# Seven half-size products for the gate and up projections of one more batch, and a new timetable

## The chip, the cores and the metric

The kernel runs on one core of a Trainium2 chip. The metric is the device time of one execution in microseconds (us). TensorE (PE) multiplies matrices into the eight banks of PSUM, VectorE (DVE), ScalarE (ACT) and GpSimd (POOL) do elementwise work, SyncE (SP) issues DMAs. Each engine takes its instructions in the order in which the program lists them; semaphores are the only tie between engines.

## The reference

The kernel computes a decoder layer of three sublayers for 4 batches of 512 tokens with 512 features, each followed by a residual sum and a layer norm: causal attention with 16 heads, the WKV recurrence over the context (a scan over the tokens, for which `k` is the first sublayer's output and `v` the context), and a gated feed-forward of 2048 hidden features with integer weights less 128, times a scale for each row.

```python
x = _layernorm(x + _L0_attn_ref(x, Wqkv, bqkv, Wo, bo))
x = _layernorm(x + _L0_xattn_ref(4, 512, 512, w, u, x, ctx_2048))
g = einsum('bsh,ih->bsi', x, Wg);  u = einsum('bsh,ih->bsi', x, Wu)
x = _layernorm(x + einsum('bsi,hi->bsh', silu(g) * u, Wd))
```

## The kernel before, in words

Every matrix product takes the float32 activations as a high and a low float16 part. `timetable()` (line 219) writes one list of pieces of work, by slots whose numbers stand in tables at the top of the file (`QK_AT`, `WKV_AT`, `WS_AT` and so on), and each engine's block walks through that list and issues its own share of every piece. So the list sets the order on every engine, and a piece whose input is late holds up all that stands behind it on its engine. Slots below 1000 lie in the attention stage. Slot 1000 + 20 b + i is in the feed-forward of batch b, after hidden tile i (0 to 15), and 1016 + 20 b + t after its y product t (0 to 3). Slots 1000 to 1007 count as 1008: the first eight tiles of batch 0 are done inside attention. A tile makes 2 ticks of the list, a y product 4, and `WAIT_IN` says how many ticks after its start a step of a chain is listed.

The feed-forward runs batch by batch: the 16 hidden tiles, then four y products of 32 matmuls.

Batches 0 and 1, the plain way: for each tile 8 matmuls of 512 columns for gate and 8 for up (`gate_up`, line 1133). ScalarE takes silu (line 1426), VectorE multiplies it with the up product (`hf`, line 1662), ScalarE and GpSimd split the result into `hh` (line 1441) and `hl` (line 1938). Their activations are `x2h` and `x2l` (lines 1359 and 1645).

Batches 2 and 3 (`SEVEN`), by seven products: the gate and up weights are stacked to one matrix and the 2 by 2 block product is done with 7 products of half-size blocks (in Winograd's form of Strassen's scheme) in place of 8. For a pair m of tiles (8 pairs) each product is 8 matmuls of 256 columns (`product`, line 1160). They need sums of weights (`weight_sum`, line 946: `WSUM`, four sums of two halves) made once, and sums of the quarters of the activations made for each batch (`quarters`: ScalarE's `x_full`, line 1364, VectorE's `x_sum`, line 1677, ScalarE's high parts, line 1377, VectorE's low parts, line 951). ScalarE copies three partial sums of each pair out of PSUM (`snap`, line 1401: snap1 before product 6, snap6 before product 7, snap5 before product 3), VectorE adds (`c11`, `c12`, `c22`, lines 1685, 1691, 1697), ScalarE takes silu (line 1408), VectorE closes with `hfb` and `hfa` (line 964), and ScalarE makes `hh` (line 1414).

Beside this run the WKV chains of later batches, four per batch: exponentials on ScalarE (lines 1323 and 1326), products on GpSimd (lines 1901 to 1918), the two scans, ekv and the division on VectorE (lines 1621, 1629, 1616, 1634), and a logarithm and an exponential (lines 1339 and 1341). Silu and these use different ACT tables, so ScalarE loads a table at each change (lines 1330, 1408, 1426). Then come `yt` with its residual and statistics (lines 1593, 1579, 1581), the second norm (line 1607) and the transposes `x2t` (line 1120). The context of a batch is loaded by SyncE (`load_ct`) to `CTS[b]`. After a y product VectorE scales and adds it (lines 1707, 1713), and ScalarE normalises it (line 1346) before SyncE writes it out (line 2088).

## Time and profile before

| what | us |
|---|---|
| median of 3 runs (lowest, highest) | 708.04 (707.57, 708.64) |
| profiled execution's own time | 711.66 |
| span of its profile | 709.9 |
| attention, to about | 375 |
| rest of batch 0's tiles and its four y products, to | 455.3 |
| batch 1's tiles, to | 515 |
| batch 1's y products, to | 544.3 |
| batch 2's tiles, to | 597.8 |
| batch 2's y products, to | 627.1 |
| batch 3's tiles, to | 676.2 |

A stage ends where TensorE issues the first matmul of the next. Matmuls overlap in the pipeline, so the pace of a stage is read from the starts of its matmuls and not from the length of one. Idle time stands in brackets behind the instruction that it precedes, with the one that ended it.

### The profile page before, as it was taken

Reading aid. Unit: us, or ns where it says so; the run is one execution under the profiler, and the core shown is the slowest. Engines: PE = TensorE matmul, PEld = TensorE weight load, DVE = VectorE, ACT = ScalarE, POOL = GpSimd, SP = SyncE. Lnnn points to the kernel's source line nnn. Section 1 sums busy time; section 2 is a strip of 40 time slices with the busy share of each in tenths; the row PEclk is TensorE's granted clock in tenths of the full one; section 3 lists DMA queues with packets and bytes.
Section 4 is the critical chain, followed back from the end, with each engine's and each line's share of the span. In section 5 each row is a group of like instructions: output and inputs, shape, how many; then the busy total and the mean of one; then the engine's idle time right before and its main releaser. Section 6 shows DMA issues by size and latency. Waiting matters only on the chain.

```text
span 709.9 us, 12525 instructions
## 1 busy us (share of the span) xinstructions
...
## 2 busy tenths in 40 slices
...
GB/s 239 249 218 235 217 145 135 98 75 79 124 102 78 38 85 163 120 143 16 8 120 60 1 0 75 16 31 0 1 1 44 17 1 2 30 31 1 1 16 45
DMA packets 45024, 54.33 MB, mean 77 GB/s; under 512 B 5921, under 2 KB 33825, under 8 KB 44961
## 3 DMA queue, kind: packets, MB, share of 16 engines
...
q10 hardware_dynamic: 432, 0.39, 0.2%
...
## 4 chain that ended last, share of the span: by engine, by line
PE 61%; DVE 13%; ACT 10%; POOL 5%; issue 5%; DMA 4%; SPq 1%; POOLq 0%; DVEq 0%; ACTq 0%
PE psb L1160 12%; PE psb L1133 8%; PE psb L996 6%; PE psb L1184 5%; PE psb L1182 5%; PE psb L1104 4%; PE psb L1072 4%; PE psb L1027 4%; DVE ee L1530 3%; PE psb L1039 3%; PE psb L1056 3%; DVE x L1607 2%; PE psb L1120 2%; PE psb L1083 2%; ACT L1330 1%
## 5 line engine op out<-in xcount | busy, mean ns | idle before, releaser
L1530 DVE CUSTOM_DVE_ANT_0 ee<-psb,mask,clip 128x512 f32<-128x512 f32 (+3 forms) x256 | 131.3, 542 | 24.9 <-PE psb L1039 22.3
L1278 ACT ACTIVATE ee<-ee,nm 128x512 f32<-128x512 f32 (+3 forms) x256 | 142.2, 560 | 1.4 <-DVE nm L1530 1.4
L1938 POOL TENSOR_TENSOR hl<-ring,hh 128x512 f16<-128x512 f32 x64 | 80.1, 1264 | 86.7 <-ACT hh L1414 57.3
L1288 ACT ACTIVATE ee<-psb 128x256 f32<-128x256 f32 (+1 forms) x192 | 94.6, 523 | 31.0 <-PE psb L1056 21.0
L1182 PE MATMUL psb<-wd,hh 128*128 128x512 f16 x240 | 91.0, 379 | 0.0
L1184 PE MATMUL psb<-wd,hl 128*128 128x512 f16 x240 | 91.0, 379 | 0.0
L1868 POOL TENSOR_SCALAR_AFFINE_SELECT ee<-ee 128x256 f32<-128x256 f32 x128 | 56.8, 452 | 60.7 <-ACT ee L1288 59.9
L1039 PE MATMUL psb<-ks,qs 128*128 128x512 f16 (+3 forms) x256 | 72.5, 305 | 8.3 <-DVE nm L1530 6.1
L1056 PE MATMUL psb<-qs,ks 128*128 128x128 f16 (+3 forms) x256 | 60.1, 306 | 9.6 <-ACT ee L1288 7.5
L996 PE MATMUL psb<-xh,wqk 128*128 128x512 f16 x240 | 61.8, 385 | 1.7 <-POOL xh L1830 1.2
L1885 POOL TENSOR_TENSOR rs<-ve,half 128x1 f32<-128x1 f32 (+1 forms) x24 | 20.5, 854 | 72.0 <-DVE ve L1599 71.7
L1278 ACT ACTIVATION_READ_ACCUMULATOR ee<-ee,nm 128x1 f32 x256 | 51.0, 199 | 0.0
L1133 PE MATMUL psb<-x2h,wg 128*128 128x512 f16 x128 | 48.6, 380 | 0.8 <-ACT ring L1426 0.5
L1133 PE MATMUL psb<-x2h,wu 128*128 128x512 f16 x128 | 48.5, 379 | 0.0
L1133 PE MATMUL psb<-x2l,wu 128*128 128x512 f16 x128 | 48.5, 379 | 0.0
L1133 PE MATMUL psb<-x2l,wg 128*128 128x512 f16 x128 | 48.5, 379 | 0.0
L1039 PEld LDWEIGHTS psb<-ks,qs 128*128 128x128 f16 x256 | 25.0, 99 | 35.6 <-DVE nm L1530 11.5
L1441 ACT ACTIVATE hh<-ring 128x512 bf16<-128x512 f32 x32 | 20.2, 630 | 30.6 <-DVE ring L1662 30.6
L1056 PEld LDWEIGHTS psb<-qs,ks 128*128 128x128 f16 x256 | 23.6, 99 | 32.1 <-ACT ee L1288 14.8
L1072 PE MATMUL psb<-ee,v 128*32 128x128 f32 (+3 forms) x512 | 37.8, 435 | 0.7 <-POOL ee L1868 0.6
L1184 PEld LDWEIGHTS psb<-wd,hl 128*128 128x128 f16 x240 | 23.4, 98 | 27.3 <-POOL hl L1938 0.2
L1182 PEld LDWEIGHTS psb<-wd,hh 128*128 128x128 bf16 x240 | 23.4, 98 | 27.2
...
## 6 DMA issues: line engine op xcount, KB each, us to landing
...
parts<-qhl SPq DMA_DIRECT2D x16, 256.0 KB, 2.2
parts<-khl SPq DMA_DIRECT2D x16, 256.0 KB, 2.2
x<-in_x SPq DMA_DIRECT2D x4, 1024.0 KB, 6.8
ct<-in_ctxT SPq DMA_DIRECT2D x4, 1024.0 KB, 5.1
out<-x SPq DMA_DIRECT2D x16, 256.0 KB, 2.0
xt<-in_xT SPq DMA_DIRECT2D x14, 256.0 KB, 3.4
```

Source lines behind the costliest of these rows:

```text
L996: mm = e.matmul(PSB[:, bk, :], wt[:, k, c0:c0 + P], xt[:, k, :], start=(p == 0 and k == 0), stop=(p == 2 and k == T - 1))
L1039: e.matmul(PSB[:, bank["score", H, i], 0:w], heads(n, "q")[:, h, i * P:(i + 1) * P], heads(n, "k")[:, h, 0:w], start=True, stop=True).then ...
L1056: mm = e.matmul(PSB[:, bk, o:o + (T - j) * P], heads(n, "k")[:, h, j * P:(j + 1) * P], heads(n, "q")[:, h, j * P:S], start=True, stop=True)
L1072: mm = e.matmul(PSB[32 * h:32 * h + 32, bk, j * P:S], VV[:, b % 2, j, g * P + 32 * h:g * P + 32 * h + 32], ET[(4 * n + h) % ET_SLOTS][:, T ...
L1133: mm = e.matmul(PSB[:, bk, :], wt[:, k, it * P:(it + 1) * P], xt[:, s, k, :], start=(k == 0 and xt is x2h), stop=(k == T - 1 and xt is x2l))
L1160: mm = e.matmul(PSB[:, bk, k * HALF_S:(k + 1) * HALF_S], weights(j, kk, 2 * m + k), moving(b, j, kk, low), start=(unit is not None and k + ...
L1182: e.matmul(PSB[:, bk, :], HS[it][0][:, t * P:(t + 1) * P], wd[:, it, :], start=(it == 0), stop=False)
L1184: mm = e.matmul(PSB[:, bk, :], HS[it][1][:, t * P:(t + 1) * P], wd[:, it, :], start=False, stop=(it == IT - 1))
L1278: e.activation(dst, dst, ACT.Exp, bias=NM[:, n % 4, col:col + 1], scale=-1.0, accum_out=DEN[:, n % 4, col:col + 1]).then_inc(sem("exp"), 1)
L1288: e.activation(ET[H % ET_SLOTS][:, base:base + width], PSB[:, bank["turn", H, item], 0:width], ACT.Exp, scale=SC).then_inc(sem("et"), 1)
L1530: e.tensor_tensor_reduce(E[H % E_SLOTS][:, EOFF[i]:EOFF[i] + w], PSB[:, bank["score", H, i], 0:w], MASK[:, S - w:S], -SC, CLIP[:, i:i + 1] ...
L1938: e.tensor_tensor(HS[it][1][:], pair(b, it // 2)[:, it % 2, :] if b in SEVEN else ring(b, it)[1], HS[it][0][:], ALU.subtract).then_inc(sem ...
```

## The change

Batch 1 joins `SEVEN`, so its 256 matmuls of 512 columns become 448 of 256 columns, with the sums and closings described above. For this the buffers are dealt anew: the quarters of batch 1 lie over `CT` (`XE[1]`, and its snap5 in `CT[:, 3, :]`), so the context of batch 3 goes to `X[0]`, batch 0's result, and is loaded only when that has been written out. The fourth sum of weights goes to `QS3` and `KS3` and no longer over `X[0]`. The sums of weights are listed in slots 1010 to 1018 (they were in 1021 to 1036), and for that the last attention output product of batch 3 in slot 1010 (it was in 1013). All tables of slots are new; those of the feed-forward stand in full below, those of attention cut to a few.

```diff
-SEVEN = (2, 3)
+SEVEN = (1, 2, 3)
-W_SPLIT = (10, 14, 17, 19)
-V0_AT = (0, 12)
+W_SPLIT = (9, 13, 13, 15)
+V0_AT = (1, 14)
-V_AT = {1: (56, 57, 58, 66), 2: (119, 127, 137, 145), 3: (178, 191, 192, 203)}
+V_AT = {1: (55, 58, 60, 69), 2: (118, 126, 139, 146), 3: (178, 191, 192, 206)}
...
-WAIT_IN = {'r1': 1, 'norm': 3, 'ek': 0, 'scan_q': 0, 'scan_p': 9, 'seed': 10, 'refine': 3, 'divide': 6, 'r2': 0,
-           'x2h': 0, 'x2l': 0, 'norm2': 7}
+WAIT_IN = {'r1': 1, 'norm': 4, 'ek': 0, 'scan_q': 0, 'scan_p': 11, 'seed': 11, 'refine': 3, 'divide': 8, 'r2': 0,
+           'x2h': 2, 'x2l': 11, 'norm2': 7}
...
-WKV_AT = {(0, 0): 124, (0, 1): 136, (0, 2): 144, (0, 3): 162, (1, 0): 204, (1, 1): 215, (1, 2): 259, (1, 3): 270,
-          (2, 0): 1003, (2, 1): 1013, (2, 2): 1017, (2, 3): 1018, (3, 0): 1020, (3, 1): 1031, (3, 2): 1035, (3,
-          3): 1040}
-YT_AT = {0: (172, 178, 185, 191), 1: (1013, 1014, 1015, 1016), 2: (1026, 1027, 1028, 1029), 3: (1045, 1046, 1047,
-         1049)}
-X2_AT = {0: (222, 225, 226, 233), 1: (1018, 1018, 1018, 1018), 2: (1036, 1036, 1037, 1037), 3: (1057, 1057, 1057,
-         1057)}
-WO_IN = (7, 8, 9, 13)
+WKV_AT = {(0, 0): 123, (0, 1): 135, (0, 2): 143, (0, 3): 162, (1, 0): 204, (1, 1): 215, (1, 2): 259, (1, 3): 270,
+          (2, 0): 1001, (2, 1): 1015, (2, 2): 1017, (2, 3): 1020, (3, 0): 1023, (3, 1): 1032, (3, 2): 1036, (3,
+          3): 1038}
+YT_AT = {0: (172, 179, 185, 191), 1: (1012, 1013, 1013, 1015), 2: (1029, 1032, 1033, 1033), 3: (1043, 1045, 1045,
+         1047)}
+X2_AT = {0: (226, 226, 230, 235), 1: (1017, 1018, 1018, 1018), 2: (1036, 1036, 1036, 1036), 3: (1055, 1055, 1055,
+         1056)}
+WO_IN = (7, 8, 9, 10)
...
-WS_AT = {1: (1025, 1028), 2: (1026, 1035), 3: (1021, 1023), 4: (1033, 1036)}
+WS_AT = {1: (1010, 1011), 3: (1014, 1017), 2: (1012, 1015), 4: (1014, 1018)}
...
     def last(b, t):
         add("norm", 2, b, t, t + 1)
         add("out", b, t)
+        if (b, t) == (0, T - 1):
+            add("load_ct", 3)
...
-    CTS = [CT, CT, CT2, CT]
+    CTS = [CT, CT, CT2, X[0]]
...
-            4: (X0H[:, 0:I], X0H[:, I:2 * I])}
-    XE = {2: CT2[:].bitcast(F16).rearrange("p t n -> p (t n)"), 3: X[1][:].bitcast(F16).rearrange("p t n -> p (t n)")}
+            4: tuple(w[:].rearrange("p k n -> p (k n)") for w in (QS3, KS3))}
+    XE = {1: CT[:].bitcast(F16).rearrange("p t n -> p (t n)"), 2: CT2[:].bitcast(F16).rearrange("p t n -> p (t n)"), 3: X[1][:].bitcast(F16).rearrange("p t n -> p (t n)")}
-    SNAP5 = [CT2[:, 3, :], YS[:, 1, :]]
+    SNAP5 = {b: (c[:, 3, :], YS[:, 1, :]) for b, c in ((1, CT), (2, CT2), (3, CT2))}
...
         if j == 4:
-            q.wait_ge(sem("out0"), 16 * T)
+            q.wait_ge(*by_turned(NG - 1))
...
+                elif b == 3:
+                    sp.wait_ge(sem("out0"), 16 * T)
                 elif b:
-                    sp.wait_ge(*by("yt", b // 2, T - 1))
+                    sp.wait_ge(*by("yt", 0, T - 1))
```

## Rows read from the trace of the kernel before

**Rows 1.** Busy us (xinstructions) of each engine by stretch.

```profile
core 0: us, PE busy (x) PEld busy (x) DVE busy (x) ACT busy (x) POOL busy (x), PEclk, DMA share, GB/s
0.00:375.00 375.00, 344.58 (x2157) 178.79 (x2158) 289.41 (x855) 310.95 (x866) 234.00 (x356) 0.98 0.48 127
...
399.60:455.30 55.70, 55.70 (x281) 27.87 (x278) 40.50 (x64) 30.95 (x47) 32.92 (x30) 1.00 0.07 25
455.30:515.00 59.70, 59.02 (x286) 28.21 (x286) 42.94 (x54) 37.83 (x51) 42.98 (x35) 1.00 0.04 14
515.00:544.30 29.30, 29.30 (x146) 14.24 (x144) 22.60 (x32) 13.65 (x20) 15.75 (x16) 1.00 0.05 19
544.30:597.80 53.50, 51.90 (x470) 45.62 (x469) 43.99 (x78) 35.86 (x60) 22.96 (x21) 1.00 0.03 11
...
627.10:676.20 49.10, 49.10 (x450) 43.66 (x449) 30.62 (x57) 30.06 (x52) 14.45 (x14) 1.00 0.02 6
```

**Rows 2.** Timeline of TensorE: start us, length us, line, operation.

```profile
500.65 0.38 PE L1133 MATMUL psb<-x2h,wg 128*128 128x512 f16 x1
...
514.46 0.60 PE L1120 MATMUL psb<-ident,x 128*128 128x128 f32 x4
...
627.09 0.27 PE L1160 MATMUL psb<-x2h,wg 128*128 128x256 f16 x1
...
676.09 0.38 PE L1182 MATMUL psb<-wd,hh 128*128 128x512 f16 x1
```

**Rows 3.** Waits of 455 to 515: us in total, times, longest.

```profile
DVE ekv L1616 <- ACT ek L1323: 2.7, 1, 2.7
DVE ct L1634 <- POOL ct L1918: 2.3, 1, 2.3
```

**Rows 4.** TensorE's idle times in batch 2's products (timeline).

```profile
...
555.68 0.39 PE L1160 MATMUL psb<-ct,woh 128*128 128x256 f16 x2 [0.32 <-ACT ys L1401]
...
559.81 0.39 PE L1160 MATMUL psb<-ct,s2a 128*128 128x256 f16 x2 [0.46 <-ACT snap L1401]
...
563.42 0.39 PE L1160 MATMUL psb<-ct,woh 128*128 128x256 f16 x2 [0.82 <-ACT ys L1401]
```

**Rows 5.** Timeline of ScalarE in the same stretch.

```profile
552.51 1.28 ACT L1408 ACT_TABLE_LOAD   x1
553.81 1.33 ACT L1408 ACTIVATE ring<-ring,g 128x512 f32<-128x512 f32 x2
...
555.64 1.28 ACT L1330 ACT_TABLE_LOAD   x1
```

**Rows 6.** Groups of VectorE in 455.3 to 515: xcount | busy, mean ns.

```profile
L1662 DVE SCALAR_TENSOR_TENSOR ring<-ring,c,psb 128x512 f32<-128x512 f32 x14 | 10.4, 745 | 9.4 <-ACT ring L1426 9.3
```

**Rows 7.** One line's instructions: the sums of weights, first and dearest.

```profile
L946 DVE TENSOR_TENSOR woh<-wg,wu x1: 2079/2079/2079, 472.0 to 472.0; 128x2048 f16<-128x2048 f16 x1
L946 DVE TENSOR_TENSOR wol<-wg,wu x1: 1217/1217/1217, 480.8 to 480.8; 128x2048 f16<-128x2048 f16 x1
```

**Rows 8.** The same view: quarter sums, their low parts, the low part removed.

```profile
L1677 DVE TENSOR_TENSOR ring<-ring x6: 682/692/693, 532.7 to 615.7; 128x512 f32<-128x512 f32 x6
...
L951 DVE TENSOR_TENSOR x2l<-ring,x2h x4: 1218/1218/1221, 535.4 to 618.2; 128x1024 f16<-128x1024 f32 x4
...
L1645 DVE SCALAR_TENSOR_TENSOR x2l<-psb,x2h x8: 678/684/691, 309.8 to 454.5; 128x512 f16<-128x512 f32 x8
```

**Rows 9.** Timeline of VectorE: its last step behind batch 0's third y product.

```profile
450.73 0.15 DVE L1599 TENSOR_SCALAR ve<-mv 128x1 f32<-128x1 f32 x1
```

**Rows 10.** The page's DMA issues: xcount, KB each, median us to landing.

```profile
ct<-in_ctxT SPq DMA_DIRECT2D x4, 1024.0 KB, 5.1
out<-x SPq DMA_DIRECT2D x16, 256.0 KB, 2.0
```

**Rows 11.** Groups of VectorE in 544.3 to 597.8.

```profile
L964 DVE SCALAR_TENSOR_TENSOR ring<-ring,c,psb 128x256 f32<-128x256 f32 x14 | 6.0, 471 | 0.5 <-PE psb L1160 0.4
...
L964 DVE SCALAR_TENSOR_TENSOR ring<-ring,c,ys 128x256 f32<-128x256 f32 x6 | 2.9, 524 | 0.0
```

More of the change, by code:

```diff
@@ L117 @@
-WO_IN = (7, 8, 9, 13)
-WD_AT = (257, 257, 258, 261)
-ZERO_IN = (1, 4, 6, 8, 9, 9, 9, 9, 9, 10, 10, 11, 11, 13, 13, 17)
-WS_AT = {1: (1025, 1028), 2: (1026, 1035), 3: (1021, 1023), 4: (1033, 1036)}
+        2, 'ek': 1, 'scan_q': 2, 'scan_p': 14, 'seed': 6, 'refine': 8, 'divide': 13, 'r2': 1, 'x2h': 0, 'x2l': 1,
+        'expand': 4}
+WAIT_IN = {'r1': 1, 'norm': 4, 'ek': 0, 'scan_q': 0, 'scan_p': 11, 'seed': 11, 'refine': 3, 'divide': 8, 'r2': 0,
+           'x2h': 2, 'x2l': 11, 'norm2': 7}
+PIECE_AT = {'load_second': 33, 'small': 70, 'split_wo': 47, 'load_ds': 180}
@@ new lines @@
+WU_AT = (41, 47, 48, 48)
+WU_ZERO = (61, 121, 121, 143)
+WG_AT = (202, 214, 221, 233)
+WG_ZERO = (220, 223, 242, 243)
+REST_AT = (7, 28, 96, 15)
+BO_AT = (53, 97, 128, 183)
+XLOAD = {1: (2, 4, 26, 30), 2: (62, 65, 88, 90), 3: (128, 132, 147, 162)}
+XSPLIT = {1: (24, 28, 32, 33), 2: (83, 84, 94, 97), 3: (145, 159, 162, 165)}
+WKV_AT = {(0, 0): 123, (0, 1): 135, (0, 2): 143, (0, 3): 162, (1, 0): 204, (1, 1): 215, (1, 2): 259, (1, 3): 270,
+          (2, 0): 1001, (2, 1): 1015, (2, 2): 1017, (2, 3): 1020, (3, 0): 1023, (3, 1): 1032, (3, 2): 1036, (3,
+          3): 1038}
@@ L361, in residual @@
                 late(wait("norm"), lambda: add("norm", 1, b, 0, T))
-                if b < 2:
-                    add("load_ct", 2 * b + 1)
+                if b == 0:
+                    add("load_ct", 1)
         for c in range(T):
@@ L1370, in x_part_high @@
                 act.wait_ge(*by("xt", b, k))
-            if k < 2:
+            if k < 2 and b == 1:
+                act.wait_ge(*by_put(NG - 1, "q"))
+                act.wait_ge(*by_put(NG - 1, "k"))
+            elif k < 2:
                 act.wait_ge(*by_gate_up(b - 2))
-            elif b == 2:
+            elif b < 3:
                 act.wait_ge(*by("yt", b, T - 1))
```

70 lines of the change are left out of this document (27 added, 43 removed), and 18 rows, old and new, of the table TURN_AT.

## The prediction, made before the changed kernel was run

> **What bounds the kernel now.** I read the busy time by stretch first. From 399.6 us, where the last tiles of batch 0 run, TensorE is busy in every microsecond but 0.7 in batch 1's tiles and 1.6 in batch 2's, at a granted clock of 1.00, the level of 2.4 GHz [rows 1]. So from there to the end the time is the number of matmul columns, and each microsecond of matmuls taken away counts, if no other engine takes TensorE's place. Up to 375 us TensorE is idle for 375.0 - 344.6 = 30.4 us, in many small waits [rows 1]. The second thing to see is how near the others are: VectorE has 40.5 of 55.7 us and then 42.9 of 59.7 (73% and 72%), but 44.0 of 53.5 (82%) in batch 2's products, where TensorE begins to wait [rows 1]. The engine that the change loads is the one that is second now.
>
> The profiled execution took 711.66 us, its span is 709.9, and the median of the runs is 708.04. All terms below are differences inside the feed-forward; I make the sum against 711.66 and take off the 3.62 between it and the median.
>
> **The products.** Before, 64 matmuls of 512 columns go from 500.65 to 514.46, 0.2158 us each; in batch 3 448 of 256 columns go from 627.09 to 676.09, 0.1094 us each [rows 2]. Batch 1 has 256 of the first kind, 55.24 us, and gets 448 of the second, 49.00 us: **-6.24**. The 0.7 us of idle time in its tiles [rows 1] belongs to the plain way (a tile waited for a bank) and goes: **-0.66**, as 59.70 - 59.02. Together -6.90. The y products, the transposes and their places between the tiles stay as many.
>
> **Stalls inside batch 1's products.** Three products of each pair wait for a copy by ScalarE. With one WKV chain in its way batch 2 lost 0.32, 0.46 and 0.82, that is 1.60 us [rows 4]: ScalarE went to load a table, 1.28 us, for silu, and again for the logarithm, while the copies stood behind [rows 5]. Batch 1's stage has three chains: (2,3) at slot 1020, (3,0) at 1023 and (3,1) at 1032. At 1.60 each that is 4.8; (2,3) begins while TensorE waits for the quarters anyway (next part), and the end of (3,1) moves into the y products, since its start behind tile 12 leaves 7 ticks in the tiles and its second scan is listed 11 after its start. So I take two, **+3.2**. The lower end is one, 1.6. The upper end is given by VectorE and is worked out with the second rival.
>
> ScalarE's own load is no bound: 37.8 us before, of which the new way replaces some 19 (silu and high parts) by batch 3's 30.1 [rows 1], so 49 in about 55.
>
> The Trainium skill ("ScalarE: Activation LUTs", section "What ACT_TABLE_LOAD costs") puts a drain of 1.38 us on top of the 1.28 us of each change of table, 2.66 in all. The row speaks otherwise: the load begins at 552.51 and the silu behind it starts at 553.81, 0.02 us after its end [rows 5]. By the page each of the four changes of two chains would cost 1.38 more and the term would be 8.7 in place of 3.2; I go by the row.
>
> **The start of batch 1's products.** New before the first product are 2 ScalarE steps and five of VectorE. Behind batch 0's third y product VectorE is free at 450.9 [rows 9]. Then come the last sum of weights (1.22) [rows 7], four sums of quarters (4 x 0.69) and the first low part (1.22) [rows 8]: 456.1, where TensorE is ready at 455.3. That is 0.8. Product 6, fourth in the order, waits for snap1, which waits for all low parts, since the last of them reads the tile that snap1 overwrites: 456.1 + 2 x 1.22 + 0.68 [rows 8] + a copy of 0.6 (ScalarE's mean in batch 3, 30.1 us over 52 [rows 1]) = 459.8, and three products of 8 x 0.1094 bring TensorE there at 458.7. That is 1.1. Together **+2.0**. Not less than 0: the quarters could be ready in time if VectorE ran ahead. Not more than 4.0, if the sums of weights listed in tiles 10 to 15 leave VectorE some 2 us behind.
>
> **The sums of weights.** Eight instructions of VectorE, two of 2.1 and six of 1.2 to 1.4, 11.7 us [rows 7], move from batch 1's and its y products' slots to 1010 to 1018. VectorE is idle for 15.2 us of the 55.7 there [rows 1], and they lie in that: 0 by themselves. Without that cover they delay the last `hf` of batch 0, then `hh` and `hl`, and y(0,0), which reads the pairs in order; that is held in the two ends of the start.
>
> **Batch 2's products.** Chain (3,3) starts two slots earlier, among y products, though its logarithm is still listed at the second tile of batch 2. I take half of its 1.60 as gone: **-0.8**, ends 0 and -1.6.
>
> **Batch 3's context.** It now waits until batch 0 is written out. In SyncE's queue it stands behind the write of y(0,3), and nothing is queued there that another engine wants earlier. Batch 0's last norm is listed after tile 1 of batch 1, about 465 us; the write takes 2.0 and the load 5.1 [rows 10], so it lands at about 473. Its reader, ekv of chain (3,0), is listed after tile 3: 457 + 2 x 6.1 + 0.4 = 470, and ScalarE's two exponentials, 1.3 us, as two silus [rows 5], and the chain before it come first: 471 to 473. **0**, with 4.0 as the upper end: VectorE would stand in its queue before `c11`, and TensorE two products behind it.
>
> **Attention.** Its pieces are the same in number and length, only slots move by up to nine. It has 30.4 us of idle time in which a move can gain or lose [rows 1], and I see no row that gives a sign: **0**, ends -3 and +3.
>
> **The sum.** -6.24 - 0.66 + 3.2 + 2.0 - 0.8 = -2.50. 711.66 - 2.50 = 709.16 for the profiled execution, less 3.62: **705.5 us** for the median.
>
> **The rivals.**
>
> *The cover holds.* The start costs nothing, and the stage no more than batch 2's did, 1.6: 708.04 - 6.90 + 1.6 - 0.8 = 701.9. For it: batch 3's 448 products ran with no gap at all [rows 1, 2]. Against it: no chains ran beside them, and VectorE had 30.6 of 49.1.
>
> *VectorE becomes the bound* (the slower side). Its work from 399.6 to 515 was 40.5 + 42.9 = 83.4 us [rows 1]. Off go 14 `hf` of 0.745 (10.4) [rows 6], four low parts of 0.68 (2.7) [rows 8] and the second scan and division of (3,1), about 2. On come the closings, batch 3's 30.6 [rows 1] less 2.5 for the y product's remainder in it, 28.1; four sums of quarters and the low parts, 2.8 + 4.3 [rows 8]; and the two sums of weights that stood behind 515, 2.6 [rows 7]. That makes 106.1, where TensorE has 115.4 - 6.9 = 108.5 left. In my forecast the stretch lasts 113.7, so VectorE may be idle for 7.6 us of it. It had forced waits of 2.7 for exponentials and 2.3 for GpSimd in batch 1's stage alone [rows 3], and in batch 2's products it was idle for 9.5 of 53.5 [rows 1]. At that share it would be idle for 10.6 in the stage, and with 1.8 more before it the stretch lasts 118.5: 3.1 more than before, less 0.8 for batch 2, 710.3. It decides from 10 us of idle time on. For it: the sum itself. Against it: much of the idle time in batch 2 was waiting for TensorE, which a late VectorE doesn't do. Its far end, everything from 399.6 at 18% idle, is beyond 713.
>
> *Batch 3's context is late.* Priced at 3 in addition to the forecast, 708.5, the same as before.
>
> *VectorE and GpSimd block each other.* Batch 1 has GpSimd busy for 43.0 us [rows 1]. Sixteen `hfb` and four low parts read two tiles of SBUF each. Its mean instruction there is 43.0 / 35 = 1.23 us [rows 1]. If each of the twenty had to wait for half of one, three times in four, that is 20 x 0.61 x 0.75 = 9, and the time 714.5. Against it: in batch 2 the `hfb` that read `YS` took 524 ns on average where `hfa`, which reads PSUM, took 471 [rows 11]; at that rate it is 1 us in all, hidden in my 3.2. The Trainium skill ("SBUF — State Buffer", section "Who interferes with whom") has such a rule: an instruction of VectorE with two SBUF inputs and one of GpSimd exclude each other for their whole length. The measured 53 ns show it to be rare here.
>
> *The attention's new slots decide*: 3 us either way, 702.5 or 708.5.
>
> **How the numbers follow.** Forecast 0.42 (704 to 707: 0.37 faster, 0.05 same), cover holds 0.15 (faster), VectorE the bound 0.22 (0.18 slower, 0.04 same), late context 0.10 (0.08 same, 0.02 slower), blocking 0.04 (slower), attention 0.07 (0.03, 0.02, 0.02). 0.2% is 1.4 us, about what a measurement can tell from no change here. Faster 0.55, same 0.19, slower 0.26. The range goes from 701.0, just under the case where the cover holds, to 711.0, just over the central price of the VectorE case; the tail of that case, blocking and an attention that gains on top of a full cover stay outside. Cases of both signs hold much of the chance; the forecast's own range is 704 to 707.
>
> **What would show it.** The spacing of the products in batch 1: 0.1094 us. Idle time before line 1160 between about 455 and 512, ended by ScalarE's copies, 3 to 4 us, most of it near table loads; the second rival shows VectorE over 93% busy there, with waits ended by lines 1685 to 1697 or 1677 and 951. The first product comes 0 to 2 us after the last y matmul of batch 0, and no gap inside y(0,0). A VectorE wait for the DMA into `x` before ekv shows the third rival. TensorE's idle time before 375 should be 27 to 33 us. The forecast is wrong if batch 1's stage, first product to first y matmul, isn't 53 to 58 us long, or if attention moves by more than 3 us.

## The result, and the profile after

| | before | after |
|---|---|---|
| median of 4 runs each (lowest, highest) | 707.81 (707.48, 708.64) | 731.1 (730.18, 731.4) |
| profiled execution's own time | 711.66 | 731.01 |
| span of its profile | 709.9 | 729.3 |

The ratio is 1.0306, with a 95% interval of 1.0281 to 1.033: the change makes the kernel 23.3 us slower, where 705.5 was predicted. The two traces differ by 19.4; the other 3.9 is that the profiled run of before lay 3.9 over its own median, while that of after is at its median. All medians are of executions at the usual clock; one execution of e3, at a mean granted clock of 0.56, took 1150.26 us and is left out.

First the stages, from the first matmul of one to the first of the next, read from TensorE's timeline; the 3.95 us of waiting ahead of batch 1's first product is counted with its tiles. "Idle" is TensorE's, "half" is the time at a granted clock of 1.2 GHz.

| stage | before: us (idle, half) | after: us (idle, half) | difference |
|---|---|---|---|
| to y(0,0) | 424.5 | 422.9 | -1.6 |
| y products of batch 0 | 30.9 (0, 0) | 30.0 (0, 0) | -0.9 |
| batch 1's tiles | 59.6 (0.5, 0) | 71.2 (14.1, 10.2) | +11.6 |
| y products of batch 1 | 29.4 (0, 0) | 34.5 (2.2, 3.4) | +5.2 |
| batch 2's tiles | 53.5 (1.6, 0) | 59.8 (5.9, 6.8) | +6.4 |
| y products of batch 2 | 29.4 (0, 0) | 28.1 (0, 0) | -1.3 |
| batch 3 | no change | no change | 0 |

In the wake of a change to one stage, three stages lost. From y(0,0) to the end the kernel before takes 285.4 us and the kernel after 306.4, so the feed-forward lost 21.0. The feed-forward repeats (e10, which has that of the kernel before, takes 285.5 us); what lies before y(0,0) doesn't. With the old tables of attention it took 424.5, 421.5 and 421.4 us in the profiled runs of the kernel before, e2 and e8, with the new ones from 419.5 to 426.4. The other 2.3 us of the 23.3 is within that scatter.

The busy time of the engines by stretch, of the kernel after (us, then each engine's busy time and instructions, granted clock of TensorE, DMA share, GB/s), says that no engine was full over a whole stage:

```profile
core 0: us, PE busy (x) PEld busy (x) DVE busy (x) ACT busy (x) POOL busy (x), PEclk, DMA share, GB/s
0.00:375.00 375.00, 347.81 (x2171) 181.10 (x2172) 290.90 (x856) 314.18 (x870) 236.38 (x358) 0.98 0.47 127
399.60:452.30 52.70, 52.68 (x265) 26.21 (x263) 47.15 (x66) 26.05 (x39) 36.36 (x27) 1.00 0.02 6
452.30:524.10 71.80, 57.75 (x480) 48.52 (x479) 57.84 (x89) 51.34 (x77) 38.50 (x35) 0.93 0.08 27
524.10:558.40 34.30, 32.03 (x154) 15.93 (x152) 26.06 (x37) 16.50 (x24) 16.28 (x17) 0.95 0.02 9
558.40:618.40 60.00, 54.13 (x479) 47.50 (x478) 44.40 (x79) 34.01 (x57) 24.62 (x23) 0.94 0.04 14
```

In batch 1's tiles TensorE has 57.8 of 71.8 us, VectorE 57.8, ScalarE 51.3, GpSimd 38.5: the fullest stands at 81%. What a reader should look for then is not the busiest engine of the stage but what each waited for. TensorE's timeline, its longest waits from batch 1 to batch 2's first pairs (start, length, operation; in brackets the idle time before it and what ended it):

```profile
456.84 0.27 PE L1161 MATMUL psb<-x2h,wg 128*128 128x256 f16 x1 [3.95 <-DVE x2l L952]
...
475.19 0.39 PE L1161 MATMUL psb<-ct,s2a 128*128 128x256 f16 x2 [1.18 <-ACT snap L1399]
...
478.80 0.39 PE L1161 MATMUL psb<-ct,woh 128*128 128x256 f16 x2 [0.82 <-ACT ys L1399]
...
487.14 0.61 PE L1161 MATMUL psb<-ct,s2a 128*128 128x256 f16 x2 [4.67 <-ACT snap L1399]
...
520.33 0.39 PE L1161 MATMUL psb<-ct,woh 128*128 128x256 f16 x2 [1.69 <-ACT ys L1399]
...
531.61 0.39 PE L1183 MATMUL psb<-wd,hh 128*128 128x512 f16 x1 [1.35 <-ACT hh L1412]
...
566.91 0.58 PE L1161 MATMUL psb<-ct,s2a 128*128 128x256 f16 x2 [5.54 <-ACT snap L1399]
```

All but the first end with one of ScalarE's copies (`snap`, line 1399 now) or parts. So the next view is ScalarE's timeline ahead of 487.14, then that of VectorE, on which ScalarE waited, and GpSimd's beside it:

```profile
482.84 1.15 ACT L1412 ACTIVATE hh<-ring 128x512 bf16<-128x512 f32 x2 [4.09 <-DVE ring L965]
484.01 1.28 ACT L1331 ACT_TABLE_LOAD   x1
485.30 0.63 ACT L1340 ACTIVATE qs_<-ek 128x512 f32<-128x512 f32 x1
485.96 0.63 ACT L1342 ACTIVATE qs_<-qs_ 128x512 f32<-128x512 f32 x1
486.50 0.58 ACT L1399 ACTIVATE snap<-psb 128x512 f32<-128x512 f32 x1
```

```profile
474.10 1.24 DVE L1614 TENSOR_TENSOR ekv<-ek,x 128x512 f32<-128x512 f32 x1 [1.12 <-ACT ek L1324]
475.26 2.17 DVE L1619 TENSOR_TENSOR_SCAN qs_<-ew,ek 128x512 f32<-128x512 f32 x1
477.36 0.66 DVE L1683 TENSOR_TENSOR ring<-psb,snap 128x512 f32<-128x512 f32 x1
477.94 2.14 DVE L965 SCALAR_TENSOR_TENSOR ring<-ring,c,ys 128x256 f32<-128x256 f32 x2
480.01 1.75 DVE L1632 SCALAR_TENSOR_TENSOR ct<-ek,ct 128x512 f32<-128x512 f32 x1
481.68 0.68 DVE L1689 TENSOR_TENSOR ring<-psb,ys 128x512 f32<-128x512 f32 x1
482.29 0.86 DVE L965 SCALAR_TENSOR_TENSOR ring<-ring,c,psb 128x256 f32<-128x256 f32 x2
```

```profile
474.75 3.64 POOL L1936 TENSOR_TENSOR hl<-ring,hh 128x512 f16<-128x512 f32 x2
...
478.51 1.29 POOL L1899 TENSOR_TENSOR x<-ek,x 128x512 f32<-128x512 f32 x1
479.88 1.33 POOL L1903 TENSOR_TENSOR ek<-ek,qs_ 128x512 f32<-128x512 f32 x1
```

This is one chain through three engines. VectorE takes ekv and a scan of chain (3,0) and the division of chain (2,3) between the closings of a pair; so `hfa` is late (482.29), ScalarE's `hh` stands first in its queue and waits 4.09 us for it, and behind `hh` stand a table load, the logarithm, the exponential and only then the copy for which TensorE waits. The order of the lists is one part of it. The other is that VectorE had no gap from 474.10 to the closing at 482.29: in these 8.2 us it was full. And four of its groups there took longer than usual, each with GpSimd at work beside it: ekv 1.24 for a median of 0.69, the scan 2.17 for 1.22, two `hfb` 2.14 for 0.96, the division 1.75 for 0.71. By these rows I estimate 3.7 us of lengthening, most of the 4.09. The sum at 477.36, with an input in PSUM and GpSimd at work beside it too, took its usual 0.66. I wrote at the top that semaphores are the only tie between the engines; by these rows they are not. e12 below says how much of it is due to GpSimd's chain work.

In batch 2 it is the same in other clothes. ScalarE's and GpSimd's timelines ahead of 566.91:

```profile
564.29 0.63 ACT L1340 ACTIVATE qs_<-ek 128x512 f32<-128x512 f32 x1 [6.03 <-POOL ek L1903]
564.95 0.63 ACT L1342 ACTIVATE qs_<-qs_ 128x512 f32<-128x512 f32 x1
565.49 0.80 ACT L1347 ACTIVATE x<-x,shift,rs 128x512 f32<-128x512 f32 x1
566.19 0.57 ACT L1399 ACTIVATE snap<-psb 128x512 f32<-128x512 f32 x1
```

```profile
552.15 1.27 POOL L1908 TENSOR_TENSOR x<-x,ps 128x512 f32<-128x512 f32 x1 [7.95 <-DVE ps L1627]
...
562.67 1.59 POOL L1903 TENSOR_TENSOR ek<-ek,qs_ 128x512 f32<-128x512 f32 x1
```

GpSimd waited 7.95 us for the second scan of chain (3,2), which stands behind the sums of quarters in VectorE's queue; the sum of chain (3,3), which now starts two slots sooner, comes 10 us later (562.67), and its logarithm is listed ahead of the first `snap`. The distance of the second scan, 11 now, is not the reason: with the old 9 GpSimd waits 7.23 us at the same place (e13).

### The profile page after: what moved, and what is told of

It reads as the page before. It is cut to its first block and busy times, and to the rows that moved or that the text cites. A ratio compares the mean times of both kernels' runs of the same rounds, so it can differ in the third digit from the quotient of the medians.

```text
span 729.3 us, 13011 instructions
## 1 busy us (share of the span) xinstructions
PE 674.1 (92%) x4482; PEld 403.8 (55%) x4482; DVE 540.2 (74%) x1264; ACT 508.0 (70%) x1167; POOL 398.5 (55%) x508
## 5 line engine op out<-in xcount | busy, mean ns | idle before, releaser
L1289 ACT ACTIVATE ee<-psb 128x512 f32<-128x512 f32 (+1 forms) x192 | 94.4, 523 | 26.3 <-PE psb L1057 17.0
L1883 POOL TENSOR_TENSOR rs<-ve,half 128x1 f32<-128x1 f32 (+1 forms) x24 | 22.3, 929 | 63.0 <-DVE ve L1597 62.8
L1412 ACT ACTIVATE hh<-ring 128x512 bf16<-128x512 f32 x48 | 27.5, 620 | 36.5 <-DVE ring L965 35.3
L1161 PE MATMUL psb<-x2h,wg 128*128 128x256 f16 x192 | 45.3, 276 | 3.9 <-DVE x2l L952 3.9
L1161 PE MATMUL psb<-x2l,wg 128*128 128x256 f16 x192 | 45.3, 276 | 0.0
L1040 PEld LDWEIGHTS psb<-ks,qs 128*128 128x128 f16 x256 | 24.9, 100 | 34.7 <-DVE nm L1528 11.2
L1185 PEld LDWEIGHTS psb<-wd,hl 128*128 128x128 f16 x240 | 23.5, 98 | 29.4 <-POOL hl L1936 2.5
L1183 PEld LDWEIGHTS psb<-wd,hh 128*128 128x128 bf16 x240 | 23.5, 98 | 28.8 <-ACT hh L1412 1.8
L1683 DVE TENSOR_TENSOR ring<-psb,snap 128x512 f32<-128x512 f32 x24 | 16.5, 689 | 27.4 <-PE psb L1161 23.3
L997 PEld LDWEIGHTS psb<-xh,wqk 128*128 128x128 f16 x240 | 22.5, 98 | 24.8 <-POOL xh L1828 2.3
```

The source lines that it names most:

```text
L997: mm = e.matmul(PSB[:, bk, :], wt[:, k, c0:c0 + P], xt[:, k, :], start=(p == 0 and k == 0), stop=(p == 2 and k == T - 1))
L1040: e.matmul(PSB[:, bank["score", H, i], 0:w], heads(n, "q")[:, h, i * P:(i + 1) * P], heads(n, "k")[:, h, 0:w], start=True, stop=True).then ...
L1161: mm = e.matmul(PSB[:, bk, k * HALF_S:(k + 1) * HALF_S], weights(j, kk, 2 * m + k), moving(b, j, kk, low), start=(unit is not None and k + ...
L1183: e.matmul(PSB[:, bk, :], HS[it][0][:, t * P:(t + 1) * P], wd[:, it, :], start=(it == 0), stop=False)
L1185: mm = e.matmul(PSB[:, bk, :], HS[it][1][:, t * P:(t + 1) * P], wd[:, it, :], start=False, stop=(it == IT - 1))
L1289: e.activation(ET[H % ET_SLOTS][:, base:base + width], PSB[:, bank["turn", H, item], 0:width], ACT.Exp, scale=SC).then_inc(sem("et"), 1)
```

## The experiments

Each kernel is the one after with the edit shown, unless another is named, and each ratio is to the kernel before on the same chip. "Tiles 1" is the stage of batch 1's tiles, with the wait ahead of its first product, "tiles 2" that of batch 2's. Where a kernel computes less, its expectation says which part. Microseconds against the kernel after are taken from its 731.1, which was measured apart; the median of the kernel before lay between 707.8 and 709.9 in the several groups of runs, so such a difference is good to a microsecond or two.

**e1_slots_plain.** The slots without the seven products.

```diff
-SEVEN = (1, 2, 3)
+SEVEN = (2, 3)
```

> The changed kernel with batch 1 done the plain way again (SEVEN = (2, 3)), all else of the change kept: new slots, sums of weights at 1010 to 1018, batch 3's context in X[0]. Theory L (load): what costs is the load of batch 1's copies, closings and quarters on VectorE and ScalarE beside the WKV chains. Then this runs at 706 to 711 us, and batch 1's tiles take about 60 us with under 1.5 us of idle TensorE. Theory S (slots): the new slots put the chains, the sums of weights and chain (3,3)'s logarithm in bad places whatever batch 1 does. Then batch 2's products keep some 6 us of idle time and slow clock, and the time is 715 us or more.

Measured 722.47, ratio 1.0196 (1.0147 to 1.0245). But part of it was made by the experiment: the plain way's low parts were listed with the wait of the new one (`x2l` 11), behind the scaling of y(0,3), which made TensorE wait 5.73 us with a lower clock behind it. e5 repeats it without that and is 7.6 us shorter.

**e2_old_slots_seven.** All the old tables except `WS_AT` and `WO_IN`, with the seven products.

```diff
-          (2, 0): 1001, (2, 1): 1015, (2, 2): 1017, (2, 3): 1020, (3, 0): 1023, (3, 1): 1032, (3, 2): 1036, (3,
-          3): 1038}
+          (2, 0): 1003, (2, 1): 1013, (2, 2): 1017, (2, 3): 1018, (3, 0): 1020, (3, 1): 1031, (3, 2): 1035, (3,
+          3): 1040}
...
```

> The changed kernel (batch 1 by seven products) with all tables of slots of the kernel before, except WS_AT and WO_IN, which have to be the new ones. Theory L: 725 us or more, batch 1's products with over 10 us of idle TensorE, since the work beside them is the same. Theory S: the old places are the better ones, 703 to 712 us.

741.97, ratio 1.0476 (1.0419 to 1.0534). Tiles 1 take 77.2 us with 17.2 idle, and y(0,0) waits 5.98 us for the down weights that ScalarE converts. Tiles 2 are as in the kernel before (53.5, 1.6 idle). So the new timetable doesn't make tiles 1 slow, since they are slower still in the old one, but what tiles 2 lost comes with the new one; e5 says so too.

**e3_one_table.** Chains of batches 2 and 3 without changes of table.

```diff
-            e.activation(SEED, EK2S[c % 2][:], ACT.Ln).then_inc(sem("seed"), 1)
+            e.activation(SEED, EK2S[c % 2][:], ACT.Ln if b < 2 else ACT.Copy).then_inc(sem("seed"), 1)
...
```

> The changed kernel with the exponentials and the logarithm of the chains of batches 2 and 3 replaced by identity and copy of the same size (so their values are wrong), so that ScalarE needs no change of table beside silu. If the table loads in ScalarE's queue are what holds back the copies out of PSUM: 8 to 14 us less than the changed kernel, 717 to 723. If VectorE's queue (closings, scans, quarters) is the bound and ScalarE only passes its lateness on: 727 to 731.

723.54, ratio 1.02 (1.0151 to 1.0249): 7.6 us of the 23.3. The wait in the middle of tiles 1 is hardly shorter, 4.31 in place of 4.67:

```profile
484.74 0.39 PE L1161 MATMUL psb<-ct,s2a 128*128 128x256 f16 x2 [4.31 <-ACT snap L1401]
```

My forecast had put the price of a chain on the table loads. That is a third of it.

**e4_chains_later.** The four chains of batch 3 later: tiles 1 have one chain beside them in place of three.

```diff
-          (2, 0): 1001, (2, 1): 1015, (2, 2): 1017, (2, 3): 1020, (3, 0): 1023, (3, 1): 1032, (3, 2): 1036, (3,
-          3): 1038}
+          (2, 0): 1001, (2, 1): 1015, (2, 2): 1017, (2, 3): 1020, (3, 0): 1036, (3, 1): 1038, (3, 2): 1042, (3,
+          3): 1047}
...
```

> The changed kernel with the chains of batch 3 later: (3,0) to (3,3) at 1036, 1038, 1042, 1047 in place of 1023, 1032, 1036, 1038, and yt of batch 3 at 1051 to 1054. Batch 1's products then have one chain beside them in place of three. Theory L: batch 1's stage gets 7 to 10 us shorter, of which batch 2's products, which get more of a chain, give back 2 to 4: 722 to 727. If the cost is the late quarters and the start of batch 1's products, or the closings by themselves: 729 to 733.

744.56, ratio 1.0491 (1.0447 to 1.0534). Tiles 1 fell from 71.2 to 59.4, and tiles 2 rose from 59.8 to 85.6. The waits that are left in tiles 1 behind the first product, with one chain, (2,3), beside them:

```profile
469.25 0.39 PE L1161 MATMUL psb<-ct,woh 128*128 128x256 f16 x2 [0.33 <-ACT ys L1399]
473.38 0.39 PE L1161 MATMUL psb<-ct,s2a 128*128 128x256 f16 x2 [0.46 <-ACT snap L1399]
476.99 0.39 PE L1161 MATMUL psb<-ct,woh 128*128 128x256 f16 x2 [0.82 <-ACT ys L1399]
```

These are the 1.6 us of the forecast, wait by wait: a lone chain costs in batch 1 what it cost in batch 2. The two further ones of the kernel after bring the idle time behind the first product from 1.6 to 10.1. In tiles 2, where one chain's first scan lay (558.9) and at whose start or within which three do now (543.3, 564.5 and 585.3), the idle time rises from 5.9 to 23.5. Not all of this is crowding: the last wait, 6.8 us, is for the second norm of batch 3, whose inputs this edit also made later.

**e5_slots_plain_x2.** e1 with the plain way's old waits.

```diff
-SEVEN = (1, 2, 3)
+SEVEN = (2, 3)
-            'x2h': 2, 'x2l': 11, 'norm2': 7}
+            'x2h': 0, 'x2l': 0, 'norm2': 7}
...
```

> As e1_slots_plain (batch 1 the plain way, all new slots), but batch 1's x2h and x2l are listed straight behind their transposes, as in the kernel before; the quarters of batches 2 and 3 keep their new place. In e1_slots_plain TensorE waited 5.7 us before batch 1's first tile for x2l, which the new WAIT_IN lists behind y(0,3)'s scaling, and the clock fell for 6.8 us. If that is an artefact of doing batch 1 plainly in these slots: 722.5 falls by 7 to 9 us to 713 to 716, and what is left above the kernel before is batch 2's 5.5 us of idle time and slow clock, due to the slots alone. If batch 1's first tile is late for another reason: 719 us or more.

714.87, ratio 1.0072 (1.0044 to 1.01). So some 5 us (by the ratio) to 6.5 (by the medians) are the new slots' own; behind y(0,0) its trace is 5.6 longer than that of the kernel before. Tiles 2 take 60.9 (53.5 before) and batch 1's y products 31.1 (29.4), 9.2 more, and the other stages gain the rest back. The wait is the very one of the kernel after, with batch 1 in the plain way:

```profile
549.53 0.58 PE L1161 MATMUL psb<-ct,s2a 128*128 128x256 f16 x2 [5.55 <-ACT snap L1402]
```

The seven products in batch 1, in these slots, cost the other 16.2 (15.4 behind y(0,0) in the traces).

**e6_last_chain.** Only chains (3,2) and (3,3) put back to where they were.

```diff
-          (2, 0): 1001, (2, 1): 1015, (2, 2): 1017, (2, 3): 1020, (3, 0): 1023, (3, 1): 1032, (3, 2): 1036, (3,
-          3): 1038}
+          (2, 0): 1001, (2, 1): 1015, (2, 2): 1017, (2, 3): 1020, (3, 0): 1023, (3, 1): 1032, (3, 2): 1035, (3,
+          3): 1040}
```

> The changed kernel with only two chains put back to their old slots: (3,2) at 1035 and (3,3) at 1040 in place of 1036 and 1038. Theory S for batch 2: the logarithm of (3,3), which ScalarE reaches before batch 2's first copy and for which it waits 6.0 us on GpSimd, causes the 5.5 us of idle time and the 6.8 us of slow clock there. Then batch 2's products take 53 to 56 us in place of 59.6, and the time is 724 to 728. If batch 2 is late since batch 1's work spills over into it: no change, 730 to 733.

734.48, ratio 1.0356 (1.0333 to 1.0379). The 5.54 before `snap` went, and 5.65 came further on, where a transpose waits for the division of the late chain. The wait moved and did not shrink.

```profile
578.48 0.87 PE L1121 MATMUL psb<-ident,x 128*128 128x128 f32 x3 [5.65 <-DVE x L1632]
```

**e7_short_after** and **e8_short_before.** Every instruction of the chains of batches 2 and 3 on 8 columns in place of 512, in the kernel after and in the kernel before: as many instructions, waits and places, but almost no work.

```diff
+    def W(b):
+        return S if b < 2 else 8
...
-            e.activation(SEED, EK2S[c % 2][:], ACT.Ln).then_inc(sem("seed"), 1)
+            e.activation(SEED[:, 0:W(b)], EK2S[c % 2][:, 0:W(b)], ACT.Ln).then_inc(sem("seed"), 1)
...
```

> The changed kernel with every instruction of the WKV chains of batches 2 and 3 on 8 columns in place of 512 (the rest of the recurrence is left out): their number, order, waits and table loads stay, their work nearly goes. Compared with e8_short_before, the same cut in the kernel before. Theory L1 (the chains' work beside the closings is what costs): the change then saves, e7 is 2 to 6 us under e8. Theory L2 (closings, copies and quarters are too much for VectorE and ScalarE by themselves): e7 is above e8 by 5 us or more.

> The kernel before with the chains of batches 2 and 3 on 8 columns (the rest of the recurrence is left out). The plain tiles and y products hid them, but for the 1.6 us in batch 2's products: 705 to 708 us under either theory.

e7: 710.68 (10 runs), ratio 1.0027 (1.0007 to 1.0047). e8: 706.99 (10 runs), 0.9972 (0.9955 to 0.9988). The chains' work costs 20.4 us in the kernel after and 1 to 2 in the kernel before. Without it the change costs 3.7.

**e9_short_one_table.** e7 and e3 together.

```diff
+    def W(b):
+        return S if b < 2 else 8
...
-            e.activation(SEED, EK2S[c % 2][:], ACT.Ln).then_inc(sem("seed"), 1)
+            e.activation(SEED[:, 0:W(b)], EK2S[c % 2][:, 0:W(b)], ACT.Ln if b < 2 else ACT.Copy).then_inc(sem("seed"), 1)
...
```

> e7_short_after (the changed kernel, chains of batches 2 and 3 on 8 columns) without their table changes too (identity and copy in place of exponential and logarithm; that part of the work is left out). In e7 TensorE still waited 6.9 us from batch 1's products to the start of its y products, most of it before reads of ScalarE's copies. If the table loads cause those waits, idle time falls to under 3 us and the time to 703 to 707, under e8_short_before's 707.0. If VectorE's queue causes them: within 1 us of e7, 709.5 to 711.5.

702.07, ratio 0.9888 (0.9847 to 0.9929), 4.9 below e8. Windows on batch 1's tiles in e9 and e8 (that of e9 runs 0.7 us into the y products, that of e8 stops 0.2 short):

```profile
454.60:507.50 52.90, 52.86 (x480) 47.11 (x481) 40.68 (x85) 32.78 (x66) 18.52 (x33) 1.00 0.10 36
```

```profile
452.10:510.20 58.10, 58.10 (x284) 28.13 (x283) 31.02 (x52) 32.22 (x48) 22.10 (x30) 1.00 0.02 5
```

From the first matmul of the tiles to the first y matmul e9 takes 52.17 us (454.61 to 506.78) and e8 58.31 (452.10 to 510.41). With nothing in their way the seven products give 6.14 of the 6.24 of the forecast; 0.7 is lost again to the wait ahead of the first one. TensorE is busy in all of it.

**e10_attention_slots.** The kernel before with the new slots below 1000 alone.

```diff
-EX_AT = {0: 21, 1: 45, 2: 58, 3: 77, 4: 89, 5: 99, 6: 123, 7: 140, 8: 155, 9: 170, 10: 189, 11: 208, 12: 214, 13:
-         235, 14: 253, 15: 261}
+EX_AT = {0: 22, 1: 45, 2: 53, 3: 80, 4: 88, 5: 105, 6: 120, 7: 138, 8: 153, 9: 171, 10: 190, 11: 206, 12: 212,
+         13: 230, 14: 253, 15: 261}
...
```

> The kernel before with the change's new slots for attention alone; the feed-forward (plain batch 1, its slots, sums and chains) is as before. The profiles showed attention 1.6 to 2.5 us shorter with the new slots. If that holds: 705 to 707 us, faster than the kernel before. If it was the scatter of single profiles: 707 to 709.

710.37 (12 runs from 706.79 to 715.46) against 709.52, ratio 1.0012 (0.9987 to 1.0037): no difference that can be told. The single runs are 8.7 us apart, more than what was asked.

**e11_fill.** Sixteen matmuls of 512 columns that nobody reads, put where TensorE waits ahead of batch 1's first product.

```diff
+            if (b, m, j) == (1, 0, 1):
+                for _ in range(16):
+                    e.matmul(PSB[:, bk, :], wd[:, 0, 0:P], wd[:, 0, :], start=True, stop=True)
```

> The changed kernel with 16 matmuls of 512 columns without use, into the bank that batch 1's first product will overwrite, ahead of its wait for the quarters (3.9 us idle there, and a clock of half speed for 3.4 us right after). They fit in the idle time. If the idle time brings on the slow clock: no slow clock between 450 and 465 us, and the first product starts no later; 1.7 us less, 728 to 731. If the slow clock comes anyway: 731 or more.

730.75, ratio 1.0285 (1.0252 to 1.0318), the same as the kernel after. The six microseconds behind the first product, in the kernel after and in e11:

```profile
456.80:462.80 6.00, 5.96 (x40) 4.77 (x41) 5.15 (x9) 1.94 (x5) 1.19 (x2) 0.72 0.23 87
```

```profile
455.90:461.90 6.00, 5.99 (x55) 5.43 (x56) 5.86 (x11) 2.95 (x6) 1.76 (x2) 1.00 0.23 87
```

The clock went from 0.72 to 1.00 and 55 matmuls ran in place of 40. The next wait then grew from 0.32 to 0.82, and y(1,0) came 0.6 us sooner after y(0,0) than without. TensorE wasn't the one that set the pace here, so its clock gave nothing in the median, and 0.6 of the expected 1.7 us in the trace. The three other stretches at the lower clock were not tested in this way.

**e12_pool_short** and **e15_vector_short.** As e7, but only GpSimd's part of the chains on 8 columns (e12), or only VectorE's (e15).

```diff
-            e.tensor_tensor(CTS[b][:, c, :], CTS[b][:, c, :], PS[:, 0:S], ALU.add).then_inc(sem("num"), 1)
+            e.tensor_tensor(CTS[b][:, c, 0:W(b)], CTS[b][:, c, 0:W(b)], PS[:, 0:W(b)], ALU.add).then_inc(sem("num"), 1)
...
```

```diff
-            e.tensor_tensor_scan(PS[:, 1:S + 1], EW[:, c:c + 1].broadcast_to([P, S]), EKV[:], 0.0, ALU.mult,
+            e.tensor_tensor_scan(PS[:, 1:W(b) + 1], EW[:, c:c + 1].broadcast_to([P, W(b)]), EKV[:, 0:W(b)], 0.0, ALU.mult,
...
```

> The changed kernel with only GpSimd's part of the chains of batches 2 and 3 on 8 columns (five products of each; that work is left out); VectorE's scans and ScalarE's exponentials stay whole. If GpSimd counts, by ScalarE's logarithm that waits for it and by blocking VectorE's instructions with two SBUF inputs: 10 to 15 us less than the changed kernel, 716 to 721. If VectorE's own scans and divisions count: under 4 us less, 727 or more.

> The changed kernel with only VectorE's part of the chains of batches 2 and 3 on 8 columns (ekv, both scans, the division; that work is left out), GpSimd and ScalarE whole. GpSimd's part alone was worth 14.0 us (e12_pool_short), both with ScalarE's 20.4. If VectorE's own time is the bound: 10 to 16 us less, 715 to 721. If the cost is ScalarE standing behind GpSimd and GpSimd's hold on VectorE: 4 to 9 less, 722 to 727.

e12: 717.13, ratio 1.0096 (1.0063 to 1.0129), 14.0 us off. e15: 717.92, 1.0103 (1.0058 to 1.0149), 13.2 us off. Together that is 27.2, where all the chain work on all three engines (e7) is 20.4; with the 7.6 of the tables (e3) 34.8, where all of it (e9) is 29.0. If one engine were full throughout, cutting another would give nothing. What each gains by stage, against the kernel after, read from the traces:

| | tiles 1 | batch 1's y products | tiles 2 |
|---|---|---|---|
| e12, GpSimd's part | 7.3 | 1.1 | 6.8 |
| e15, VectorE's part | 8.4 | -0.9 | 6.6 |
| e3, the tables | 4.0 | 2.4 | 1.8 |
| e7, all work, tables kept | 13.7 | -0.1 | 7.4 |
| e9, all work and tables | 18.3 | 2.2 | 7.9 |

In tiles 1 the parts nearly add up: 7.3 and 8.4 to 13.7, and with 4.0 to 18.3. That is how a serial chain behaves: each link takes its own length off. In tiles 2 either part alone removes the one wait of 5.54 (0.40 and 0.58 are left of it), so it is counted twice; the surplus of the sum is there. The long wait of tiles 1 in e12 and e15 (4.67 in the kernel after):

```profile
480.14 0.51 PE L1165 MATMUL psb<-ct,s2a 128*128 128x256 f16 x2 [2.29 <-ACT snap L1403]
```

```profile
479.36 0.61 PE L1165 MATMUL psb<-ct,s2a 128*128 128x256 f16 x2 [3.08 <-ACT snap L1403]
```

ScalarE's wait for `hfa` ahead of it goes from 4.09 to 1.72 and 2.51, so TensorE's wait is this one plus 0.57 or 0.58 in all three. In e12 VectorE's work in this stretch is the same, but it takes 5.8 us from ekv to `hfa` (469.48 to 475.29) in place of 8.2, with ekv, `hfb` and the division at their usual lengths:

```profile
469.48 0.69 DVE L1618 TENSOR_TENSOR ekv<-ek,x 128x512 f32<-128x512 f32 x1 [1.12 <-ACT ek L1328]
...
473.07 1.10 DVE L969 SCALAR_TENSOR_TENSOR ring<-ring,c,ys 128x256 f32<-128x256 f32 x2 [0.22 <-ACT ring L1410]
474.08 0.69 DVE L1636 SCALAR_TENSOR_TENSOR ct<-ek,ct 128x512 f32<-128x512 f32 x1
```

So 2.4 of the 4.67 us are VectorE's instructions lengthened beside GpSimd's chain work. The scan is still 2.18 in e12, beside `hl`, which was not cut.

**e13_old_steps.** The old distances of a chain's steps.

```diff
-WAIT_IN = {'r1': 1, 'norm': 4, 'ek': 0, 'scan_q': 0, 'scan_p': 11, 'seed': 11, 'refine': 3, 'divide': 8, 'r2': 0,
+WAIT_IN = {'r1': 1, 'norm': 4, 'ek': 0, 'scan_q': 0, 'scan_p': 9, 'seed': 10, 'refine': 3, 'divide': 6, 'r2': 0,
...
```

> The changed kernel with only the delays of the chains' later steps as before: second scan 9 ticks behind the start in place of 11, logarithm 10 in place of 11, division 6 in place of 8. In batch 2's start GpSimd waited 8 us for the second scan of (3,2), listed behind the quarters, and ScalarE 6 us on GpSimd. If the longer delays string the chains out into the products: 720 to 726, batch 2's 5.5 us gone. If the starts of the chains count and not the delays: 729 to 734.

732.28, ratio 1.0307 (1.0269 to 1.0346): no change. The wait in batch 2 is there, 5.70. How the steps of a chain are spread, by so little, doesn't matter; when a chain starts moves the waits (e4, e6).

**e14_in_y_stages.** An attempt at a faster version: chains start in the y products or right ahead of them, but for (3,3) in tiles 2, so that none runs through the middle of tiles 1. `WAIT_IN` is that of e13, and batch 3's `yt` is listed at 1056.

```diff
-          (2, 0): 1001, (2, 1): 1015, (2, 2): 1017, (2, 3): 1020, (3, 0): 1023, (3, 1): 1032, (3, 2): 1036, (3,
-          3): 1038}
+          (2, 0): 1001, (2, 1): 1013, (2, 2): 1016, (2, 3): 1019, (3, 0): 1034, (3, 1): 1036, (3, 2): 1038, (3,
+          3): 1052}
...
```

> The changed kernel with chains beside y products rather than beside batch 1's: (2,1) to (2,3) at 1013, 1016, 1019, (3,0) to (3,3) at 1034, 1036, 1038, 1052, yt of batch 3 at 1056, and the old delays. If the chains' place is all: batch 1's products take 55 to 60 us, batch 2's 52 to 56, and the time is 705 to 715. If there is no room left for them anywhere (e4_chains_later gained 12 us in batch 1 and lost 26 in batch 2): 720 or more, with batch 3's quarters late.

750.9, ratio 1.0567 (1.0526 to 1.0608), the slowest of all. One wait for `snap` in tiles 1 is 8.8 us long and one in tiles 2 9.7; that chains crowded into the y products wait for each other is my reading, and no run isolates it. Batch 3's second norm is late here too, by 4.7. No version that I ran with the whole computation beats the kernel before; e8 and e9, which do, leave chain work out.

## Why the prediction was wrong, point by point

**What bounds the kernel.** I had it that "from there to the end the time is the number of matmul columns, and each microsecond of matmuls taken away counts, if no other engine takes TensorE's place" [rows 1]. The condition was the wrong one: over the stage no engine took TensorE's place (81% is the fullest), a chain across engines did.

**The products, -6.24 and -0.66.** Right. In batch 1 with no chain work and no tables in the way (e9) they take 6.14 us less than in the like kernel before, with TensorE busy throughout. (59.70 - 59.02 is 0.68 and not 0.66; and 0.8 and 1.1 of the start are 1.9 and not 2.0. Neither matters.)

**The start, +2.0.** The first product waited 3.95, at the end that I had given (4.0), but not for its reason. VectorE ran the last sum of weights from 447.54 and was free then; it waited for ScalarE:

```profile
447.65 0.63 ACT L1340 ACTIVATE qs_<-ek 128x512 f32<-128x512 f32 x1 [7.39 <-POOL ek L1903]
448.31 0.63 ACT L1342 ACTIVATE qs_<-qs_ 128x512 f32<-128x512 f32 x1
448.85 1.55 ACT L1359 ACTIVATE ring<-psb 128x512 f32<-128x512 f32 x3
```

```profile
450.43 3.27 DVE L1675 TENSOR_TENSOR ring<-ring 128x512 f32<-128x512 f32 x3 [1.68 <-ACT ring L1359]
453.73 0.69 DVE L1675 TENSOR_TENSOR snap<-ring 128x512 f32<-128x512 f32 x1
454.34 2.35 DVE L952 TENSOR_TENSOR x2l<-ring,x2h 128x1024 f16<-128x1024 f32 x2
```

A logarithm of chain (2,2) stood before the quarters and waited 7.39 us for GpSimd; three sums took 3.27 in place of 2.08 (3 x 0.693); and the first product needs two low parts and not one. Where GpSimd's chain work is cut (e12) the sums take 2.13, and the start falls to 0.70. The 1.1 for snap1 didn't come.

**Stalls inside batch 1's products, +3.2.** This is the step that failed: "At 1.60 each that is 4.8 ... So I take two, **+3.2**." Measured are 14.05 - 3.95 = 10.1 us of idle time. The 1.60 was read from batch 2, where one chain runs alone beside the products [rows 4, 5], and as the price of a lone chain it was right: e4, with one chain beside batch 1's products, has 0.33, 0.46 and 0.82. What failed is to multiply it. With three chains the other two cost 8.5, not 1.6 each or nothing: steps of two chains and of a pair stand in the same queues, a step that is late holds the next engine's queue, and VectorE, full for 8.2 us ahead of the longest wait, is lengthened by GpSimd on top. e3 shows that the tables, on which I had put the price, are a third of the loss, and e12 and e15 that GpSimd's and VectorE's part each weigh more. Of the 25.6 us between forecast and measurement, tiles 1 make 13.3 (6.9 by this term, 2.0 by the start, 4.0 by the clock), tiles 2 7.2 and batch 1's y products 5.2; the other stages give 3.8 back, and 3.7 is the place of the profiled runs against their medians.

**The clock, not in the sum.** Before, TensorE had the 2.4 GHz level in all of the feed-forward's stages [rows 1]. After, it has the 1.2 GHz level from 457.7 for 3.4 us, 485.0 for 6.8, 532.8 for 3.4 and 563.5 for 6.8; ahead of each it had been idle for 3.95, 4.67, 2.2 (1.35 and 0.84) and 5.54. It had work for 3.4, 4.7, 2.6 and 3.4 us of these, and half of it, 7.0 us, is lost: 4.0 in tiles 1, 1.3 in the y products behind, 1.7 in tiles 2. With these the stages close: tiles 1 are -6.9 + 14.1 + 4.0 = +11.2 (measured +11.6). This is bookkeeping and not a test: where e11 took the first of these stretches away, 0.6 us came of its 1.7.

**VectorE as the bound (the rival of the slower side).** Its work sum was right: 106.1 forecast, 47.15 + 57.84 = 105.0 measured from 399.6 to 524.1, and "It decides from 10 us of idle time on" was the right point to watch: VectorE was idle for 19.5 us. But its price, 710.3, assumed the idle share of batch 2, and its sign in the trace (over 93% busy) didn't come. It was full for single stretches, as ahead of 487.14, and not for the stage; what held TensorE up is latency through three engines, of which such a stretch is a link.

**VectorE and GpSimd block each other.** I gave it 0.04. It is there, and in the longest wait of tiles 1 it is the largest link (2.4 of 4.67 by e12). In the kernel after, minimum, median and maximum in ns:

```profile
L965 DVE SCALAR_TENSOR_TENSOR ring<-ring,c,ys x24: 473/478/1483, 477.9 to 696.8; 128x256 f32<-128x256 f32 x24
...
L1675 DVE TENSOR_TENSOR ring<-ring x9: 682/693/1755, 450.4 to 629.4; 128x512 f32<-128x512 f32 x9
```

and in e12, GpSimd's chain work cut:

```profile
L969 DVE SCALAR_TENSOR_TENSOR ring<-ring,c,ys x24: 473/479/485, 473.1 to 681.4; 128x256 f32<-128x256 f32 x24
...
L1679 DVE TENSOR_TENSOR ring<-ring x9: 682/692/693, 448.0 to 614.0; 128x512 f32<-128x512 f32 x9
```

The long ones of these two lines are gone; the scans still reach 2181, beside `hl`. The Trainium skill ("SBUF — State Buffer", section "Who interferes with whom") has the rule, and I set it aside by a mean of 53 ns [rows 11], taken where GpSimd had few instructions. The medians still say so; the few long ones stood in the chain that counted. The maxima of before would have warned me: its two scans took up to 2871 and 2293 ns for a median of 1220. Its share of the whole 14.0 of e12 stays open, since the cut also shortens GpSimd's own steps. No run takes the lengthening away alone.

**Batch 2, -0.8.** Measured +6.4: 4.3 more idle time, 1.7 by the clock, and 0.4 with 8 transposes more. The slots alone do it (e5), and the wait goes when (3,2) and (3,3) get their old places (e6), though another comes for it. I had taken an earlier start for a gain and not looked at what the chain's steps then stand behind.

**Batch 1's y products, not in the sum.** +5.2: `hh` and `hl` of the last pairs come late (1.35, 0.84 and smaller ones), the clock, and 8 transposes more (24 for 16), while batch 2's y products have 12 fewer (4 for 16). I had kept their places. e7 has these waits too, 34.6 us; e9 has 32.3.

**Batch 3's context, 0.** Right: the load was issued at 466.68 and ekv at 474.10 waited only for `ek`. **Sums of weights, 0**, and **attention, 0**: -1.6 up to y(0,0) in the traces and no difference that e10 can tell; idle time before 375 is 375.0 - 347.8 = 27.2. The table load took 1.28 us again, and the next operation came 0.01 behind it (484.01, 485.30); the drain that the Trainium skill adds ("ScalarE: Activation LUTs", section "What ACT_TABLE_LOAD costs") isn't seen.

What stays open: how much of the link that GpSimd makes is its own time and how much VectorE's lengthened instructions, outside the one wait that is shown; what the three stretches at the lower clock that e11 left would give back; and whether some other placement of eight chains carries the seven products. That the slots and the products together make 6.5 + 16.2 is a split in one order only, since the old slots with the products (e2) fail for a reason of their own.
